# The MLP of each batch computed inside the loop of hyperbolic attention

## The reference, cut to what matters

```python
# hyperbolic attention, 16 heads of 8, over the 256 tokens of one batch
cosh_arg = maximum(1 + 2 * (|q|^2 + |k|^2 - 2 q.k) / denom, 1)
attn = softmax(-arccosh(cosh_arg))          # x = x + (attn @ v) @ wo.T
# MLP, width 512, on each token by itself
h = relu(layernorm(x) @ w1 + b1)
x = x + h @ w2 + b2
```

## Time and profile before

| | |
|---|---|
| median of 3 executions | 2583.7 us (2578.2 to 2590.47) |
| profiled execution, first to last instruction | 2563.6 us |
| what the median has beyond that span | 20.1 us |
| busy over the span | PE 81%, VectorE 78%, ScalarE 72%, GpSimd 65% |
| mean granted TensorE clock | 0.844 |

### The profile page before, as it was taken

One profiled execution on the slowest core, in us unless ns is written; L12 is line 12 of the kernel. 1 busy time (PEld: TensorE's weight loads), 2 busy tenths in 40 slices (PEclk: granted clock), 3 DMA queues, 4 the chain that ended last, 5 costly groups with the idle time before them and its releaser, 6 DMA issues. The chain is left out here.

```text
span 2563.6 us, 50172 instructions
## 1 busy us (share of the span) xinstructions
PE 2079.1 (81%) x14935; PEld 1515.9 (59%) x14935; DVE 1998.1 (78%) x6007; ACT 1854.7 (72%) x3188; POOL 1663.5 (65%) x1516
## 2 busy tenths in 40 slices
PE   4999999999999979999947666666666666666599
PEld 4777777777777668888834444443433444434266
DVE  4677777777777757877768999999999999999522
ACT  2666666666666634344239999999999999999743
POOL 2767766676667400000058999999999999999600
PEclk7999999999999969999966677777777777777599
DMA  5000000000000024334200000000000000000011
GB/s 136 1 2 2 1 1 0 1 0 1 1 0 1 2 67 108 93 92 110 68 1 1 1 1 0 0 0 0 0 0 0 0 0 0 0 0 1 7 31 37
DMA packets 44067, 49.03 MB, mean 19 GB/s; under 512 B 5112, under 2 KB 27038, under 8 KB 43934
## 3 DMA queue, kind: packets, MB, share of 16 engines
q1 hardware_dynamic: 35614, 43.32, 7.0%
q10 hardware_dynamic: 8320, 4.19, 0.7%
HBM read 42.78 MB, written 4.72 MB: 19 GB/s over the span
## 5 line engine op out<-in xcount | busy, mean ns | idle before, releaser
L1460 POOL TENSOR_TENSOR u<-u,spare 128x1024 f32<-128x1024 f32 x256 | 597.2, 2372 | 35.1 <-ACT spare L1433 34.9
L545 ACT ACTIVATE prob<-s_ps,nmax 128x128 f32<-128x128 f32 (+1 forms) x1024 | 364.4, 432 | 140.1 <-DVE nmax L602 140.0
L1353 PE MATMUL d_ps<-rowsT 28*128 28x256 f32 x1024 | 165.9, 404 | 331.3 <-DVE u L1532 331.2
L602 DVE CUSTOM_DVE_ANT_0 s_ps<-s_ps,mask 128x128 f32<-128x128 f32 (+1 forms) x1024 | 341.3, 385 | 101.8 <-issue 77.9
L1353 PEld LDWEIGHTS d_ps<-rowsT 28*128 28x128 f32 x1024 | 106.2, 242 | 430.4 <-issue 430.0
L582 POOL TENSOR_TENSOR g_lo<-g_all,g_hi 128x512 fp32r<-128x512 f32 x256 | 329.1, 1286 | 21.4
L1528 DVE TENSOR_SCALAR u<-d_ps 128x1024 f32<-128x1024 f32 x256 | 311.9, 1218 | 39.5 <-PE i_ps L1353 39.3
L1532 DVE SCALAR_TENSOR_TENSOR u<-i_ps,u 128x1024 f32<-128x1024 f32 x256 | 313.5, 1225 | 14.8
L1471 POOL TENSOR_TENSOR spare<-spare,u 128x1024 f32<-128x1024 f32 x128 | 303.1, 2368 | 10.7
L1447 ACT ACTIVATE u<-u 128x1024 f32<-128x1024 f32 x256 | 258.3, 1070 | 0.0
L1450 ACT ACTIVATE u<-u 128x1024 f32<-128x1024 f32 x256 | 257.5, 1066 | 0.0
(11 more groups left out here) (265 smaller groups left out, 5577.9 us busy)
## 6 DMA issues: line engine op xcount, KB each, us to landing
w_all<-w_rows SPq DMA_DIRECT2D x128, 256.0 KB, 5.6
x<-L_attn_x ACTq DMA_DIRECT2D x8, 512.0 KB, 14.0
y<-y_rows SPq DMA_DIRECT2D x16, 256.0 KB, 2.3
wkqv<-L_attn_Wkqv SPq DMA_DIRECT2D x4, 528.0 KB, 8.7
gate_rows<-L_ffn_gate_proj SPq DMA_DIRECT2D x1, 512.0 KB, 14.5
up_rows<-L_ffn_up_proj SPq DMA_DIRECT2D x1, 512.0 KB, 11.5
down_cols<-L_ffn_down_proj SPq DMA_DIRECT2D x1, 512.0 KB, 13.3
w_rows<-wT SPq DMA_DIRECT2D x8, 64.0 KB, 1.6
```

The source lines that it names most:

```text
L545: last = nc.scalar.activation(prob[:, kind, at, :].rearrange("p c n -> p (c n)"), s_ps[kind][:, at.start * P:at.stop * P], ACT.Exp, bias=n ...
L602: last = nc.vector.tensor_tensor_reduce(out=scores, in0=scores, in1=keep.mask[:, N - width:N], scale=-1.0, scalar=3.4e38, op0=ALU.add, op1 ...
L1353: last = nc.tensor.matmul(ps[:, e * W2 + j * N:e * W2 + (j + 1) * N], rowsT[at, slot(i, p), 1, j * P:(j + 1) * P], rowsT[at, slot(i, p), 0 ...
L1460: nc.gpsimd.tensor_tensor(u[:, slot(i, p), :], u[:, slot(i, p), :], spare[:, p % SPARE, :], ALU.add).then_inc(sum_done, 1)
```

## The change

The stage `mlp` and the `rstd_of_all` before it go. `hyperbolic_attention` becomes `hyperbolic_attention_and_mlp`. Body b of each engine now also carries the MLP of batch b - 4 (its moments, scale and normalised tile: batch b - 3; its last addition: batch b - 5), on 256 tokens. b1 is folded into row 127 of w1, whose row of the transposed input is set to one; b2 comes in as a matmul with one row. `r_ps` and half of `o_ps` serve as its PSUM. The first two turns of the loop are written out instead of one. The sum lands in `keep.x`, and SyncE stores each batch (128 KB) from there. The preparation of `b1T` in `load_and_fold` goes.

```diff
+        def pe_turn_x4(pe, b, i, rows_read):
+            pe.wait_ge(xh4_done, (b + 1) * TB)
+            pe.wait_ge(rowsT_done[0], rows_read)
+            after(pe, relu_done, 2 * b)
+            for j in range(TB):
+                last = nc.tensor.transpose(r_ps[0][:, j * P:(j + 1) * P], xh4[:, i, j, :], keep.ident)
+            last.then_inc(x4_turned, 1)
+        def pe_hidden(pe, b, half, rows_read):
...
+            pe.wait_ge(xT4_done, b + 1)
+            if half == 0:
+                pe.wait_ge(rowsT_done[1], rows_read)
+                after(pe, relu_done, 2 * b - 1)
+            for n in range(HW):
+                w = half * HW + n
+                last = nc.tensor.matmul(r_ps[1 - half][:, n * N:(n + 1) * N], w1[:, w * P:(w + 1) * P], xT4[:, :], start=True,
+                                        stop=True)
+            last.then_inc(h_ready, 1)
+        def pe_y(pe, b, copies):
+            pe.wait_ge(o_copied, copies)
+            pe.wait_ge(relu_done, 2 * (b + 1))
+            after(pe, y_done, b)
+            for j in range(TB):
+                out = o_ps[:, N + j * P:N + (j + 1) * P]
+                nc.tensor.matmul(out, ones_row[:, :], keep.biases[0:1, R_B2:R_B2 + P], start=(j == 0), stop=False,
+                                 skip_group_check=True)
+                for w in range(WB):
+                    last = nc.tensor.matmul(out, hidden[:, w, j * P:(j + 1) * P], w2[:, w, :], start=False,
+                                            stop=(w == WB - 1), skip_group_check=True)
+            last.then_inc(y_ready, 1)
...
+        def act_std4(act, b, i):
+            act.wait_ge(var_done, (b + 1) * TB)
+            nc.scalar.activation(std4[:, i, :], part_mv[:, i, :, 1], ACT.Sqrt, bias=eps[:, 0:1]).then_inc(std4_done, 1)
+        def act_xT4(act, b):
+            act.wait_ge(x4_turned, b + 1)
+            after(act, h_ready, 2 * b)
+            nc.scalar.copy(xT4[0:P - 1, :], r_ps[0][0:P - 1, 0:N]).then_inc(xT4_done, 1)
+        def act_relu(act, b, half):
+            act.wait_ge(h_ready, 2 * b + half + 1)
+            after(act, y_ready, b)
...
+            nc.scalar.activation(dst, r_ps[1 - half][:, :], ACT.Relu).then_inc(relu_done, 1)
...
+        def dve_rstd4(dve, b, i):
+            dve.wait_ge(std4_done, b + 1)
+            nc.vector.reciprocal(rstd4[:, i, :], std4[:, i, :]).then_inc(rstd4_done, 1)
...
+        def dve_y(dve, b):
+            dve.wait_ge(y_ready, b + 1)
...
@@ TensorE: start of the stage, body, last lines of step p @@
+                pe_fold_w1(pe)
...
+                        if four_before and p == TURN_X4_AT:
+                            pe_turn_x4(pe, b - 4, (i - 4) % TURN, (b + 1) * (HP // 2))
+                        if four_before and p == HIDDEN_AT:
+                            for half in range(2):
+                                pe_hidden(pe, b - 4, half, (b + 1) * (HP // 2))
+                        if four_before and p == HP - 1:
+                            pe_y(pe, b - 4, 2 * b)
@@ ScalarE, body @@
                         if one_after and p in (0, 2):
                             act_hi(act, b + 1, p // 2)
+                        if four_before and p == 0:
+                            act_xT4(act, b - 4)
+                        if four_before and p == 2:
+                            for half in range(2):
+                                act_relu(act, b - 4, half)
                         if two_after and p == 4:
                             act_norm(act, b + 2)
+                    if three_before:
+                        act_std4(act, b - 3, i)
                     for p in range(HP):
                         act_roots(act, b, p, i)
@@ VectorE, body @@
                         dve_ratio(dve, b, p, i)
                         if p == 0 and three_before:
                             dve_residual(dve, b - 3)
+                        if p == 0 and five_before:
+                            dve_y(dve, b - 5)
...
                         if p == 5 and three_before:
-                            dve_keep_moments(b - 3)
+                            dve_rstd4(dve, b - 3, i)
+                        if p == 6 and three_before:
+                            dve_norm4(dve, b - 3, i)
...
                             if p == 4:
+                                after(dve, relu_done, 2 * (b - 4) + 1)
                                 dve_features(dve, b + 1)
```

More of the change, by code:

```diff
@@ L1574, in turn @@
                     known = isinstance(b, int)
-                    body(b, i, not known or b >= 1, not known or b >= 2, not known or b >= 3, not known or b + 1 < batches,
-                         not known or b + 2 < batches)
+                    before = lambda n: not known or b >= n
+                    behind = lambda n: not known or b + n < batches
+                    body(b, i, before(1), before(2), before(3), before(4), before(5), behind(1), behind(2))
             whole = batches // TURN
-            turn(0, TURN)
-            with engine.Fori(1, whole) as r:
+            for r in range(2):
+                turn(r, TURN)
+            with engine.Fori(2, whole) as r:
                 turn(r, TURN)
@@ L1644, in _ @@
                 copy_rows(act, 0, ROWS_BY_SCALAR[0], 0)
+                act_fold_w1(act)
                 def weights(b, i, p):
@@ new lines, in _, with dve_moments @@
+                last = lambda b: b % TURN
+                def dve_moments(b):
+                    dve.wait_ge(res_done, b + 1)
+                    dve_stats(b, last(b))
+                    dve.wait_ge(stats_done, (b + 1) * TB)
+                    dve_aggregate(b, last(b))
+                dve_y(dve, END - 4)
+                dve_residual(dve, END - 2)
+                dve_moments(END - 2)
+                for j in range(TB):
+                    dve_normalise(dve, END - 1, j)
+                dve_residual(dve, END - 1)
@@ new lines, in _ @@
+                dve_moments(END - 1)
+                dve_y(dve, END - 3)
+                for n in range(2):
+                    dve_copy_o(dve, END, n, last(END))
+                for b in (END - 2, END - 1):
+                    dve_rstd4(dve, b, last(b))
+                    dve_norm4(dve, b, last(b))
+                for j in range(TB):
+                    dve_normalise(dve, END, j)
+                dve_residual(dve, END)
+                dve_moments(END)
+                dve_y(dve, END - 2)
@@ L1889, in _ @@
-                over_pairs(sp, pairs, body)
-                for i in range(2):
-                    sp.wait_ge(stored[i], 16 * pairs)
+                row = lambda ap: ap.rearrange("(a n) -> a n", a=1)
+                sp.dma_start(w1_rows[:, :], io["L1_ffn_w1"]).then_inc(weights_in, 16)
+                sp.dma_start(zsum[:, :], io["consts"][:, C_ZSUM:C_ZSUM + P]).then_inc(weights_in, 16)
+                sp.dma_start(last_row[:, :], io["consts"][0:1, C_LAST:C_LAST + P]).then_inc(weights_in, 16)
```

282 lines of the change are left out of this document (121 added, 161 removed).

## The result

The changed kernel takes **2879.72 us** (median of 4, 2877.46 to 2883.11) beside 2587.09 us for the kernel before in the same series: 1.112 times as long, interval 1.1085 to 1.1157. Forecast were 2675 us and a range of 2590 to 2750, so the direction was right and the size was not; the time is that of rival C. The medians differ by 292.6 us. The profiled execution has a span of 2875.6 us, 312.0 more than the one before, and a mean clock of 0.78; of the kernel before it was a short execution that was profiled (an execution's time stands 1.8 us above its span in these runs, so that one took about 2565).

The account below looks back on a forecast made before the run. It took a ring of waits across engines to bound the attention loop, at 41.0 us a batch against 34.2. Loop +190, start +1, end +30, removed stage -130 gave +91: 2583.7 + 91 = 2675 us, range 2590 to 2750.

Parts of the forecast that it names:

- rival C: Attention loop: ring holds with TensorE at the lower clock, 47.8 us a batch, 2870 us; chance 0.08 for over 2750.
- The ring: Attention loop: the MLP's steps wait on each other across ScalarE, TensorE and VectorE in a closed chain, 41.0 us a batch.
- the four places named: Loop waits: ScalarE before copy and first relu, 2-4 us each; VectorE before reciprocal, 3-4; GpSimd's single wait, about 8.
- rival A: Attention loop absorbs the MLP in TensorE's free time; ScalarE's list decides at 35.1 us a batch, 2510 us; chance 0.14.
- D: Rival: only a short ring through ScalarE and TensorE binds the loop, 38.1 us a batch, 2594 us; chance 0.05.
- the middle of 39.1 and 42.8: Loop period taken as 41.0 us, between TensorE all at full clock and a mix of full and half clock.
- step 7: Late loop-body step on TensorE: row groups 3 and 4, projection, then the w2 product; 3.6 us at full clock.
- step 2 with handovers: Loop-body step on TensorE: pairs, value group 0, q k v, MLP transposes; 2.3 us at full clock plus 0.3 handovers.
- step 2 of the ring: TensorE issues value group 1, then the hidden halves: 1.0 + 1.72 us at full clock, twice that at half.
- step 5: VectorE from waiting for ScalarE's root to the first row copy: 8.0 us, with 0.65 of new work.
- 28 x 6.8 = +190: Loop growth in us: bodies 4 to 31 carry the MLP, each 41.0 us instead of 34.2.
- ends +31: Outside the steady loop: start +1 us for folding b1, end +30 us for the last batches' MLP (20 to 45).

Follow-up runs that it names:

- e3: Changed kernel with TensorE issuing the two hidden halves ahead of value group 1, same instructions; 2791.01 us, 1.088 times the kernel before.
- e8: e7 with the MLP work placed anew so no step waits for the same body's late part; 2583.87 us, 1.007 times the kernel before.
- e7: Changed kernel with e2, e3 and normalisations over 127 columns together; 2726.0 us, 1.062 times the kernel before.
- e12: Changed kernel with an unread accumulator output added to the two normalisations; 2835.66 us, 1.097 times the kernel before.
- e2: Changed kernel with VectorE's reciprocal moved one loop step later, from 5 to 6; 2861.88 us, 1.115 times the kernel before.
- e11: e8 with the normalisations one body later, where GpSimd has no work, and everything behind them one batch later; 2577.32 us, 0.998 times the kernel before.
- e13: e11 with the two relu moved between ScalarE's pairs and the transposed tile's copy moved to VectorE; 2569.91 us, 0.993 times the kernel before.
- e4: Changed kernel with 14 unread transposes added where TensorE waits, ahead of value group 1; 2857.55 us, 1.114 times the kernel before.
- e9: Changed kernel with 14 unread transposes in each of two loop steps, 3 and 4, where TensorE waits; 2867.67 us, 1.109 times the kernel before.

## Why the prediction was right and wrong

**Right: what bounds the change.** The ring was there, with the waits at the four places named, in the order named. Free time on TensorE (11.7 us) did not help: rival A fell with e3, where the order alone moved 3.2 us, and D fell with VectorE's wait of 4.31 us at the reciprocal.

**Wrong: the level of TensorE on the ring.** The step that failed is "with more work in the list full clock should come more often. I take the middle of 39.1 and 42.8". More work came with more waiting, and the clock went from 0.70 in the loop to 0.63. The ring of the trace beside that of the prediction, in us, for the turn shown and as the mean of 20 turns:

| step | forecast | 2012.57 to 2062.66 | mean |
|---|---|---|---|
| 1 copy, pairs 2 and 3 | 4.3 | 4.2 | 4.2 |
| 2 value group 1, hidden | 2.7 full, 5.4 half | 5.1 | 5.4 |
| 3 relu | 0.7 | 0.5 | 0.5 |
| 4 pairs 4 to 7, table, root | 10.1 | 10.1 | 10.1 |
| 5 VectorE to the row copy | 8.0 | 10.1 | 10.1 |
| 6 step 7 and y | 3.6 full | 8.4 | 6.5 |
| 7 add y, pairs 1 and 2 | 7.1 | 7.1 | 7.1 |
| 8 step 2 with handovers | 2.6 full, 4.7 half | 4.5 | 4.6 |
| sum | 39.1 full, 41.0 taken | 50.1 | 48.5 |

TensorE's three steps take 16.4 us on average, with their handovers, where the 41.0 us held 10.8 (41.0 - 30.5, and 0.3 of handovers): 5.6 of the 7.5 us by which the period is longer than forecast. The levels that the prediction read off the old trace failed in step 2 of the ring: value group 1 and the hidden halves, taken at full, run at the lower level or near it in every turn. y was sorted rightly for seven turns of nine, but its price is a second error, of size: priced by its passes at 2.24 us, it takes 3.1 at the upper level and 5.45 at the lower (2045.37 to 2050.82), where from start to start its four bias passes cost 0.36 us each and its 16 others 0.25, for 0.22 by twice the price. The bound of 47.8 stood in rival C with a chance of 0.08. It deserved more: the only window of step 7 showed a clock of 0.51, and no row showed a wait that raised the clock. That the time comes out as C's is in part luck: C had TensorE at the lower level throughout, which y is not, and had nothing of the next error, which makes up for it.

**Wrong: a term of step 5.** "Two normalisations, 0.34 each, 0.52 together" came from a stage in which GpSimd does nothing. In the loop they take 2.79 us. That is the 2.1 us by which step 5 is long. The Trainium skill (Perfetto Trace Analysis, Optimization Strategy) says that interleaving two regimes may improve performance; here it cost 11%, and came back to about the old time in e8, when the ring was taken out.

**The sum.** Forecast 28 x 6.8 = +190, ends +31, stage -130: +91. Measured by spans: the loop +405.1 (383.4 and the 21.7 of its last body), which is 28 x 14.5; the end +22.2 (forecast +30, range 20 to 45), the start 0, the stage -130, and 14.7 ahead of the changed code: +312.0. The ends were right, if in the low part of their range; the period was not.

**What the experiments say of the cause.** Shown: the ring (e3, e7, e8), the wait of the normalisations for GpSimd (e12, e2, e11, e13), that the idle work tried does not lift the clock of the whole ring (e4, e9). Not shown: what the chip goes by when it grants the level, so also why y falls to the lower level in e2, e3 and e4 and not in e7, and why the sums come first in just eight batches of e13.

## What to carry to other kernels

Where strict lists of several engines are locked together, free time says little; follow one batch's new steps round the engines, and price every TensorE step on that way at the lower clock until a row shows otherwise. Take an operation's duration from a place with the same neighbours: VectorE's `tensor_scalar` in SBUF cost four times as much beside GpSimd's sums. And put new steps into such a loop so that each reads what the previous body finished: that, not the amount of work, made a period of 48.5 us into 37.8 (ratios 1.121 and 1.007 in one series), and filling ScalarE's last waits made it 36.3. A place that is free beside another engine has to be looked at again once something else gets faster, as e13 shows.

## What was not expected of the hardware

- A 128x128 `tensor_scalar` on VectorE, 0.34 us, stood up to 2.4 us while GpSimd added 128x1024 (2.33 us each), always until just after a sum ended; the profile shows this as busy time of VectorE, not as a wait. With an accumulator output it took 0.40 + 0.08 in the same place. An odd row length (127) did not free it.
- TensorE's clock in this loop with waits behaved like a seesaw: 14 idle transposes a batch took the hidden products from 613 to 392 ns and y's from 324 to 441, and 28 did no better. Moving one reciprocal (e2) took y from 3.7 to 5.5 us.
- The root behind the stages ahead of the changed code starts at 1291 us in the trace of the kernel before and at 1304 to 1319 in those of the others, mostly by `causal_attention`, whose code is the same. With kernels that differ by less than 1%, the part after a common mark tells more than the whole time.
